# Feed-forward lag of the local transformer blocks: 7 to 10 tiles behind attention instead of 8 to 11, with a drain of nine tiles

## The reference, cut to what matters

```python
def local_block(x, Wqkv, q_scale, k_scale, Wo, g, b, W1, b1, W2, b2):
    q, k, v = split(shift_tokens(x) @ Wqkv, 3)          # heads of 64 features
    q, k = rotary(l2norm(q) * q_scale), rotary(l2norm(k) * k_scale)
    x = x + windowed_softmax_attention(q, k, v) @ Wo     # window and the one before it
    a, gate = split((layernorm(shift_tokens(x)) * g + b) @ W1 + b1, 2)
    return x + (a * gelu(gate)) @ W2 + b2                # hidden width 341
```

## Time and profile before

| | before |
|---|---|
| median of 3 runs | 4953.68 us (4953.31 to 4957.55) |
| the profiled execution | 4955.57 us, its span 4953.8 us |
| TensorE busy | 91% |
| VectorE, ScalarE, GpSimd busy | 79%, 64%, 56% |
| mean share of the DMA engines, first queue | 41.1% |
| mean granted TensorE clock | 0.965 |

### The profile page before, as it was taken

One profiled execution on the slowest core, in us unless ns is written; L12 is line 12 of the kernel. 1 busy time (PEld: TensorE's weight loads), 2 busy tenths in 40 slices (PEclk: granted clock), 3 DMA queues, 4 the chain that ended last, 5 costly groups with the idle time before them and its releaser, 6 DMA issues. The chain is left out here.

```text
span 4953.8 us, 221717 instructions
## 1 busy us (share of the span) xinstructions
PE 4504.5 (91%) x82384; PEld 3376.7 (68%) x82384; DVE 3893.3 (79%) x8000; ACT 3191.7 (64%) x6750; POOL 2786.9 (56%) x4109
## 2 busy tenths in 40 slices
PE   4568969999999999999999999999998686999997
PEld 3556746777777777777777777777776454666666
DVE  6985577888888888888888888888886665777775
ACT  2004547777777777777777777777776444777776
POOL 0012147666666666666666666666664334555555
PEclk7998989999999999999999999999999688999999
DMA  2001144555555555555555555555554003444443
GB/s 79 1 1 32 41 108 126 151 137 145 139 144 140 145 139 140 142 138 145 135 151 130 153 138 146 137 149 134 149 135 105 14 11 100 116 115 117 118 115 91
DMA packets 705090, 563.74 MB, mean 114 GB/s; under 512 B 223748, under 2 KB 630120, under 8 KB 704264
## 3 DMA queue, kind: packets, MB, share of 16 engines
q1 hardware_dynamic: 691336, 537.36, 41.1%
q10 hardware_dynamic: 13312, 22.02, 1.4%
HBM read 359.38 MB, written 200.02 MB: 113 GB/s over the span
## 5 line engine op out<-in xcount | busy, mean ns | idle before, releaser
L2285 POOL TENSOR_TENSOR L_qk<-L_cos_part,L_sin_part 128x512 f32<-128x512 f32 x896 | 1129.5, 1275 | 104.9 <-DVE L_sin_part L2137 101.1
L1872 ACT ACTIVATE L_squares<-L_ps_q 128x512 f32<-128x512 f32 x896 | 536.7, 599 | 786.4 <-PE L_ps_q L1596 779.9
L1596 PE MATMUL L_ps_q<-L_w_qkv,L_xT 128*128 128x512 f32 x1792 | 977.1, 627 | 7.7 <-DVE L_sin_part L2137 3.5
L2276 POOL TENSOR_TENSOR L_qk<-L_qk,L_rnorm 128x1024 f32<-128x1024 f32 (+1 forms) x512 | 865.0, 1689 | 17.8 <-POOL L_rnorm L2259 0.5
L1632 PEld LDWEIGHTS L_ps_t<-L_ident,L_qk 128*128 128x128 f32 x3584 | 440.9, 141 | 488.1 <-issue 350.6
L2136 DVE TENSOR_TENSOR L_cos_part<-L_ps_q,L_rot 128x512 f32<-128x512 f32 x896 | 609.8, 681 | 49.5 <-ACT L_squares L1872 48.4
L2137 DVE TENSOR_TENSOR L_sin_part<-L_ps_q,L_rot 128x512 f32<-128x512 f32 x896 | 609.2, 680 | 0.0
L2138 DVE TENSOR_REDUCE L_sumsq<-L_squares 128x8 f32<-128x512 f32 x896 | 604.8, 675 | 0.0
L1632 PE MATMUL L_ps_t<-L_ident,L_qk 128*128 128x128 f32 x3584 | 543.9, 275 | 3.9 <-POOL L_qk L2276 2.2
L1883 ACT ACTIVATE L_qkT<-L_ps_t 128x512 f32<-128x512 f32 x896 | 533.2, 595 | 15.2 <-PE L_ps_t L1632 15.1
L2253 POOL TENSOR_TENSOR L_nw_a<-L_rnorm 128x32 f32<-128x32 f32 (+1 forms) x256 | 59.9, 234 | 849.5 <-ACT L_rnorm L1902 849.5
(11 more groups left out here) (299 smaller groups left out, 8939.5 us busy)
## 6 DMA issues: line engine op xcount, KB each, us to landing
L_val<-v_rows SPq DMA_DIRECT2D x896, 260.0 KB, 4.0
v_rows<-L_val SPq DMA_DIRECT2D x384, 260.0 KB, 2.1
v_rows<-L_val SPq DMA_DIRECT2D x512, 65.0 KB, 2.0
L_rot_base<-in_rot SPq DMA_DIRECT2D x256, 128.0 KB
x_rows<-z SPq DMA_DIRECT2D x144, 128.0 KB, 1.9
v_rows<-L_val SPq DMA_DIRECT2D x128, 130.0 KB, 2.0
L_x_in<-x_rows SPq DMA_DIRECT2D x512, 32.0 KB, 1.7
mid_rows<-z SPq DMA_DIRECT2D x256, 64.0 KB, 1.6
```

What stands on the lines that cost most here:

```text
L1596: nc.tensor.matmul(ps_q[j % 2][:, :], xT[:, parity(t), :], w_qkv[:, 0:2, 256 * j:256 * j + 256], start=True, stop=True).then_inc(S["proj_p ...
L1872: nc.scalar.activation(squares[:, j % 2, :], ps_q[j % 2][:, :], ACT.Square).then_inc(S["sq_done"], 1)
L2276: nc.gpsimd.tensor_tensor(v, v, r, ALU.mult).then_inc(S["normed"], 1)
L2285: nc.gpsimd.tensor_tensor(qk[:, t % 2, h, s, :], cos_part[:, j % 2, :], sin_part[:, j % 2, :], ALU.add).then_inc(S["added"], 1)
```

## The change

Four lags become smaller by one, the drain one step shorter, and three places that depend on them follow: the table `FINISH_AT`, and the steps at which the feed-forward weights of the next block are loaded. `load_group` and `store_group` are placed by the lags and so fall on even steps now instead of odd ones. `load_group` for a pair comes at step t0 + 6, directly behind `store_mid` of the pair's second tile.

```diff
-    TO_LN, TO_FT, TO_UP, TO_DOWN = 8, 9, 10, 11
-    TAIL = 10
+    TO_LN, TO_FT, TO_UP, TO_DOWN = 7, 8, 9, 10
+    TAIL = 9
@@
-        FINISH_AT = {0: (0, 1), 1: (2, 3), 2: (4, 5), 3: (6, 7), 4: (8, 9), 5: (10, 11), 6: (12,), 7: (13,), 8: (14,), 9: (15,)}
+        FINISH_AT = {0: (0, 1), 1: (2, 3), 2: (4, 5), 3: (6, 7), 4: (8, 9, 10), 5: (11, 12), 6: (13,), 7: (14,), 8: (15,)}
@@
-                        if T == 8 and more and not first_of_all(k):
+                        if T == TO_LN and more and not first_of_all(k):
                             load_up(k)
-                        if T == 9 and more and not first_of_all(k):
+                        if T == TO_FT and more and not first_of_all(k):
                             load_down(k)
```

## The result

| | median us | runs (lowest to highest) | ratio to before, 95% interval |
|---|---|---|---|
| before | 4953.84 | 15 (4951.48 to 4958.84) | 1 |
| changed | 4965.6 | 15 (4961.23 to 4972.26) | 1.0026 [1.0019, 1.0033] |

The changed kernel is 11.8 us slower. The forecast was no change (4955.8 us, 2 us over before). The profiled execution of the changed kernel has a span of 4963.4 us, against 4953.8 us before, so its account has to explain 9.6 us.

What follows compares the result with a forecast made beforehand. TensorE's own work was taken to bound L0, and with short waits L1. L0: +1.65 - 1.7 + 0 = 0; L1: +1.13 - 3.0 + 1.0 + 3.0 = +2.1; 4953.7 + 2.1 = 4955.8 us, range 4947 to 4966.

Steps and rivals of the forecast that it cites:

- The down weights in L0: L0, step 8: loads 1.03 us later behind SP's wait, covered by 1.17 us of slack, in 11 batches: 0 us.
- Rival 2: Store that SP waits for lands late where weights load, delaying L0's down weights and `f_in`: 4977 us; chance 0.13.
- Its second half: L0: `f_in` late by 0.8 us behind the output weights in 14 batches, 11 us more; whole rival's chance 0.13.
- The down weights in L1: L1: down weights 1.03 us later, delaying VectorE's product and TensorE's weighted values in 3 batches: +3.0 us.
- Parity at the borders: Block borders: scales (step 1) and output weights (step 4) meet other steps; 0, bounds -1 to +1 us for each of 14 batches.
- The drains: Both drains: logarithm starts 5.3 us after the last addition, gaining 1.7 us in L0 and 3.0 in L1.
- the down group in front of the last output projection: L0's drain: one more group of transposes and down projection on TensorE before that projection, +1.65 us.
- The second term: L1's drain: VectorE's `f_in` store and load come 1.03 us later with no slack left, +1.0 us once.
- The other steps: Steady part: SP stands 1.03 us longer in every pair, catches up, and `f_in` keeps slack: cost 0.
- Rival 3: Block borders gain: GpSimd's wait for scales is covered by layer-norm steps, up to half of 13.9 us: 4949 us; chance 0.10.
- Rival 1: Drain gets a whole step shorter in both stages, 11.8 us each, -23.6 us: 4930 us; chance 0.06.
- Rival 4: L1: SP's wait is absorbed, VectorE's wait for down weights disappears behind gelu, -4 us: 4951.8 us; chance 0.10.

Runs made afterwards that it cites:

- both edits: Changed kernel with down weights issued ahead of load_group and TensorE's L1 loop over two steps started at the odd step; 4948.6 us, ratio 0.9991 to before.

## Why the prediction was wrong

The time is 9.8 us over the forecast: just inside the range, but a slowdown that is beyond the measurement's uncertainty, to which I gave 0.15. Two steps failed in this direction, and a third, mis-sized the other way, hid part of it.

**The down weights in L0: the step that failed.** I had 1.17 us of slack against 1.03 us of delay and put 11 x 0 us. The delay was wrong. The load leaves 3.12 us after the store, and it left 0.69 us after it before, so the down weights are 2.4 us later, not 1.03; less the slack that is 1.3 us. The product stood for them in all 11 batches, 2.0 us on average, and the batch grew by 1.0. The landing of 1.70 us came from the drain and was backed by a median over 256 stores, while the step that mattered is a loaded one. In the landing records of the kernel before the store's median in L0 is 1.57 us at most steps, but 3.18 us at step 9, one step behind the up weights, and 2.8 and 3.3 us at steps 1 and 2. I never looked at the store by step. Why it lands late there stays open, as said above; that it does, and that the down weights stood behind it, is what cost the time. Rival 2 set the point from which this decides at 1.84 us and priced 2.7 us at 0.9 us a batch. It measured 2.88 us and 1.0 us a batch (0.9 by taking the down weights out of the way). Its mechanism is what happened, at a chance of 0.13. Its second half, `f_in` late behind the output weights, did not happen: with the down weights first the L0 batch is 260.86 us, 0.2 us over before, and in the changed kernel VectorE never waits for `f_in` in L0 ahead of its drain.

**The down weights in L1:** +3.0 us predicted. The runs with the down weights behind and in front of the loads differ by 1.2 us a batch, 3.7 us for three. The Trainium skill's page DMA: Bandwidth & Descriptors (section Rules for kernel authors: issue early, wait late) pointed the right way, and the reordered kernel follows it. The fixed cost of about 2 us that this page of the Trainium skill gives (section Latency and other measured facts) is over the 1.57 us of most stores here and under the 2.88 us of the one that counted. The L1 term was nearly right in sum, though made of a wait of 2.30 us and not 1.70.

**Parity at the borders: the second step that failed.** I took 0, bounds -1 to +1 us a batch, and listed scales and output weights. What parity changed was where TensorE's loop has its edge, 1.3 us in each of L1's batches. It was open to me: the helper `paired_bodies` with its one projection drawn ahead is in the code, and the change turns the pieces from odd to even. It is none of the pieces that I named. In the steady batches those stayed inside my bounds: with both edits 0.2 us a batch is left in L0 and 0.5 in L1, where ordinary pairs are even shorter than before (24.47 against 24.53 us), so that what is left stands at the batch's border. VectorE's loop also runs over two steps and kept its edge, and no run moves it.

**The drains: the mechanism was half right.** In L1 it came out in this pair of traces: the logarithm 5.47 us after the last addition (5.3 predicted), 2.9 us of gain against 3.0; the chain shrank by 2.5 us. The close match is in part luck. The chain takes 21.6 to 24.7 us in four traces with the old lags in L1 and 18.9 to 21.7 us in ten with the new ones, some 2.2 us less on average, and the kernel before stands near the long end.

In L0 I had -1.7 for the chain, and it gave 3.9. The logarithm gave 1.55 of it. The rest is TensorE's clock. These are the last up projection's first half in the kernel before, then in the changed one, from the busy time by stretch:

```profile
3852.12:3855.60 3.48, 3.48 (x8) 2.52 (x9) 0.48 (x1) 1.63 (x2) 0.00 (x0) 0.50 0.02 5
```

```profile
3857.46:3859.23 1.77, 1.77 (x9) 1.46 (x10) 0.00 (x0) 1.63 (x2) 0.00 (x0) 1.00 0.26 74
```

Before, the engine had stood from 3848.58 to 3850.72 us, and the transposes and these products ran at a granted clock of 0.50 (the lower of the two levels, 1.2 GHz). In the changed kernel the engine stood from 3849.62 to 3853.43 us, and what runs at 0.51 behind that gap is the down group of the pair before last, off the chain. The up projection has the full 2.4 GHz: 1.77 us for 3.48 in its first half and 1.03 for 1.60 in its second, 2.3 us together. The chain is 16.3 to 16.5 us in nine traces with the new lags and 18.1 in two; with the old ones it is 19.4 to 22.5 in three.

And the down group in front of the last output projection, which I charged with +1.65 us, came with something larger leaving: L0's last step up to that projection became shorter, 13.69 to 10.15 us.

```profile
3826.47:3840.16 13.69, 9.36 (x168) 7.95 (x166) 3.97 (x14) 6.81 (x12) 1.57 (x8) 0.88 0.10 25
```

```profile
3836.91:3847.06 10.15, 6.86 (x171) 6.17 (x171) 2.52 (x6) 3.62 (x6) 0.00 (x0) 1.00 0.03 8
```

TensorE is busy 9.36 of 13.69 us there, so, other than in the steady part, it isn't the only bound. Three things make up the 3.5 us. The up projections left the step (3829.38 to 3832.14, 2.76 us) and the down group came (3839.82 to 3841.54, 1.72 us), 1.0 us. TensorE no longer stands 1.00 us for gelu in front of the weighted values. And the last output projection ran at a granted clock of 0.56 before, in a step in which TensorE had stood four times, 4.3 us in all, and runs at 1.00 now, 1.45 us less:

```profile
3836.65 3.47 PE L1696 MATMUL L_ps_q<-L_w_out,L_outT 128*128 128x128 f32 x16 [0.78 <-ACT L_outT L1891]
```

```profile
3845.00 2.02 PE L1696 MATMUL L_ps_q<-L_w_out,L_outT 128*128 128x128 f32 x16 [0.78 <-ACT L_outT L1891]
```

The 1.00 us is ScalarE's part. In the kernel before that step held the gelus with both table loads, in front of the copy for the last output, for which ScalarE itself then stood 1.33 us waiting for TensorE:

```profile
3829.76 1.28 ACT L2017 ACT_TABLE_LOAD   x1
...
3831.55 1.19 ACT L1991 ACTIVATE L_gate<-L_ps_o,L_b_up 85x256 f32<-85x256 f32 x3
3832.75 1.28 ACT L2022 ACT_TABLE_LOAD   x1
...
3835.91 0.60 ACT L1891 ACTIVATE L_outT<-L_ps_t 128x512 f32<-128x512 f32 x1 [1.33 <-PE L_ps_t L1651]
```

Now up projections and gelus are a step earlier. I had counted the up projections in front of the last output (unchanged) and not asked in which step they stand. The last step repeats: it is 10.15 to 10.28 us in eleven traces with the new lags and 13.7 to 14.4 us in three with the old. But the step in front of it doesn't: 16.5 us in the changed kernel, 16.8 to 18.6 us in the other ten with the new lags, 14.4 to 17.3 us with the old. The two together take 28.0 us on average with the new lags and 30.2 us with the old, so the gain is some 2 us rather than 3.5. In L1 I had charged +1.13 + 1.0 for the drain. The second term is not there: VectorE waited 0.34 us for `f_in` where it had waited 0.28. Its last part, from the addition at 4791.73 us in the changed kernel to the last, is 145.6 us against 142.7, +2.9, with the third wait for the down weights in it. It takes 142.4 to 145.3 us in the traces with the old lags in L1 and 140.4 to 145.6 us in those with the new, so I can't split that further.

**The other steps.** SP stands longer in every pair, and in ordinary pairs this costs nothing, as predicted: with the down weights first no reader of `f_in` is late in L0 ahead of the drain, and L0's batch is 0.2 us over before. Rival 3 had its mechanism and not its gain. GpSimd's wait for the scales went from 13.9 us in 12 times to the three times of L1,

```profile
POOL L_rot L2295 <- DMA L_qk_scales<-in_L_ffn_k_scale: 3.4, 3, 1.2
```

and no batch got shorter by it: with the down weights first L0's is 0.2 us over before. Rival 1, a whole step less, did not occur in L1; in L0 the two gains together come to 7.4 us, about a third of its 23.6 us. Rival 4 did not occur.

**The sum, in the end,** in the profiled execution. L0: +10.2 (ten batches) +0.4 (up to the first of them) -4.2 (the last one with the drain: the eleventh load, and -3.5 in the last step) -3.9 (chain) = +2.6, where I had 0. L1: +2.5 (down weights in two batches) +4.0 (edge) +2.9 (left by both edits, 1.8 up to the twentieth addition and 0.5 in each of two batches, which I can't name) +2.9 (last part, with the third load) -2.5 (chain) = +9.8, where I had +2.1. The terms are rounded. Those of the steady batches are firm; the first and last parts of a stage differ by 1 to 5 us among traces with the same lags, so this sum holds for this pair of traces.

## What to carry to other kernels

Read the duration of a transfer at the step at which it will be waited for, not its median: here it was 1.57 us in most steps and nearly twice that at the one that counted, and 11 batches paid for it. Ahead of a wait on an in-order queue, issue whatever doesn't need the wait: that one reordering was worth 12 us, the whole loss, on the median. When a shift by an odd number of steps meets a loop that runs over two, the loop's edge meets other work, so ask for each engine what now stands behind the edge. And a drain is not the steady part at a lower load: before charging an instruction there at its duration, ask what leaves the same step, what each engine waits for in it, and at which granted clock it runs.

## What was not expected of the hardware

- The same 64 KB store landed in 1.57 us in most steps and in 2.88 us at step 8. In 14 traces, each of L0's 345 tile stores that followed a value store within 1.1 us took 2.59 us or more.
- Leaving out 1028 small packets a batch (690,698 packets in all instead of 705,090) brought the store at step 8 to 2.02 us, though their transfers had been issued until 2076.30 us and the store went out at 2086.66 us. The distance to the value store changed as well, so what did it is open.
- In a drain, a gap of some 2 us on TensorE (3848.58 to 3850.72 us) was followed by products at half the granted clock, and which products stood behind the gap decided 2.3 us of the chain. The last output projection took 3.47 us at a granted clock of 0.56 and 2.02 us at 1.00.
- Removing a wait of 1.9 us in all from the bounding engine's list in L1 (3 times, before the down products) shortened the stage by 0.2 us.
